# Gate's sizes taken in place while up runs, signed values by way of DRAM, first loads of u issued by ScalarE

## The reference, cut to what matters

```python
x = act_qdq(x)
up = act_qdq(x @ lpbq_dequant(w_up).T)
gate = act_qdq(x @ lpbq_dequant(w_gate).T)
sig = fixed_qdq_u16(sigmoid(gate))
gate = act_qdq(gate * sig)
o = act_qdq(gate * up)
return o @ lpbq_dequant(w_down).T
```

## Time and profile before

| | us |
|---|---|
| median of 3 runs | 1608.95 (1607.89 to 1610.02) |
| profiled execution | 1608.93 |
| its span | 1607.1 |
| PE busy | 1395.7 (87%) |
| VectorE busy | 1231.8 (77%) |
| ScalarE busy | 911.3 (57%) |
| moved by DMA | 200.56 MB, mean 125 GB/s |

### The profile page before, as it was taken

How to read it: one execution, slowest core, us unless ns; L and a number is a source line. 1 busy time by engine, 2 the same in 40 slices (tenths; PEclk the granted TensorE clock), 3 DMA queues, 4 the chain that set the end, 5 groups by cost and what they waited for, 6 DMA issues and landing times.

```text
span 1607.1 us, 24370 instructions
## 1 busy us (share of the span) xinstructions
PE 1395.7 (87%) x9268; PEld 788.3 (49%) x9268; DVE 1231.8 (77%) x1934; ACT 911.3 (57%) x1956; POOL 320.9 (20%) x326
## 2 busy tenths in 40 slices
PE   4579999999999999976999999999999203999999
PEld 3356666666666666642444444444444101444444
DVE  7657788888898988746888777688899799745641
ACT  2657787777777778755222222799844696321210
POOL 1124444444444444530111111000000000000000
PEclk9879999999999999978999999999999656999999
DMA  5101111111122221101233332577754995544532
GB/s 203 66 20 63 49 63 63 59 61 62 65 78 80 66 80 54 41 34 53 98 123 116 116 119 98 186 248 248 247 178 170 360 339 185 203 136 160 193 132 79
DMA packets 81812, 200.56 MB, mean 125 GB/s; under 512 B 7712, under 2 KB 7712, under 8 KB 78752
## 3 DMA queue, kind: packets, MB, share of 16 engines
q1 hardware_dynamic: 81696, 199.00, 35.4%
HBM read 128.72 MB, written 70.25 MB: 124 GB/s over the span
## 4 chain that ended last, share of the span: by engine, by line
PE 47%; issue 5%; DVE 1%; DMA 1%; ACT 0%; SPq 0%; POOLq 0%; POOL 0%
PE ffn_banks L1117 30%; PE ffn_banks L1135 16%; DMA ffn_ring<-sigs_dram 1%; PE ffn_banks L1093 1%; DVE ffn_wide L1283 0%; DVE ffn_rises L1288 0%; DVE ffn_peaks L1290 0%; DVE ffn_wide L1282 0%; ACT ffn_rest L1175 0%; ACT ffn_ring L1166 0%; DVE ffn_wide L1421 0%; DVE qg L1383 0%; ACT qg L1175 0%; SPq L1002 0%; PE ffn_banks L1123 0%
## 5 line engine op out<-in xcount | busy, mean ns | idle before, releaser
L1117 PE MATMUL ffn_banks<-ffn_wide,ffn_rest 128*128 128x512 f16 x2304 | 506.2, 381 | 10.4 <-DVE ffn_wide L1283 6.1
L1117 PEld LDWEIGHTS ffn_banks<-ffn_wide,ffn_rest 128*128 128x128 f16 x2304 | 226.1, 98 | 281.1 <-issue 17.3
L1135 PE MATMUL ffn_banks<-ffn_rest,ffn_wide 128*128 128x512 f16 x1152 | 251.2, 382 | 97.0 <-DVE ffn_wide L1428 97.0
L609 ACT ACTIVATE qg<-score_banks,neg_max 128x128 f32<-128x128 f32 (+1 forms) x512 | 207.6, 445 | 53.1 <-DVE neg_max L516 53.1
L1135 PEld LDWEIGHTS ffn_banks<-ffn_rest,ffn_wide 128*128 128x128 f16 x1152 | 113.2, 98 | 235.0 <-issue 100.7
L1175 ACT ACTIVATE ffn_rest<-ffn_banks,ffn_row_back 128x1024 f32<-128x1024 f32 x72 | 79.7, 1107 | 157.1 <-PE ffn_banks L1117 147.4
L1254 ACT ACTIVATE ffn_u_steps<-ffn_ring,ffn_scales 128x1024 int16<-128x1024 f32 x48 | 55.0, 1148 | 158.5 <-DMA ffn_ring<-ups_dram 131.2
L413 POOL TENSOR_TENSOR qg<-qg,per_sum 128x512 f32<-128x512 f32 x64 | 70.1, 1095 | 308.5 <-DVE per_sum L520 308.5
L415 POOL TENSOR_TENSOR qg<-qg,per_sum 128x1024 f32<-128x1024 f32 x64 | 121.1, 1892 | 0.0
L609 ACT ACTIVATION_READ_ACCUMULATOR qg<-score_banks,neg_max 128x1 f32 x512 | 118.9, 232 | 0.0
L657 PE MATMUL ring_banks<-xt,attn_hi 128*128 128x256 f16 x512 | 89.6, 277 | 10.3 <-DVE ct L501 6.3
(11 more groups left out here) (184 smaller groups left out, 2701.6 us busy)
## 6 DMA issues: line engine op xcount, KB each, us to landing
ups_dram<-ffn_rest SPq DMA_DIRECT2D x48, 512.0 KB, 3.1
ffn_ring<-ups_dram SPq DMA_DIRECT2D x48, 512.0 KB, 4.1
ffn_wide<-ups_dram SPq DMA_DIRECT2D x17, 1024.0 KB, 8.0
gates_dram<-ffn_rest SPq DMA_DIRECT2D x24, 512.0 KB, 2.7
ffn_ring<-gates_dram SPq DMA_DIRECT2D x24, 512.0 KB, 4.5
ffn_rest<-w_parts_dram SPq DMA_DIRECT2D x36, 256.0 KB, 4.0
x_in<-in_x SPq DMA_DIRECT2D x16, 512.0 KB, 3.7
qg<-in_ctxt SPq DMA_DIRECT2D x16, 512.0 KB, 4.2
```

What stands on the lines that cost most here:

```text
L609: last = act.activation(prob[:, s % 2, h, lo:hi], score_banks[:, h, lo:hi], ACT.Exp, bias=neg_max[:, s % 2, part, h:h + 1], accum_out=row_ ...
L1117: last = pe.matmul(banks[:, pair_of(s), half, :], w[:, m % 2, wp, c, :], xq[:, xp, n, c, :], start=(k == 0), stop=(k == 3 * DC - 1))
L1135: last = pe.matmul(down_banks[:, g % 2, t, :], oq[:, g % 2, op, m, t * P:(t + 1) * P], w_down[:, wp, wk, c], start=(start and k == 0), sto ...
```

## The change

`sizes` moves into the second pass and works in place on `qg`. A double's signed values are first stored to a new DRAM tensor, `signs` (`store_signed`, in SP's slot after the one in which the double's odd piece is made, ahead of that slot's fetches and of the store of up), and ScalarE takes the sizes one slot after that (`size_slots`). Double 23 keeps its signs and is the only one with two products. The signed values come back pair by pair and piece by piece (`load_signed`): those of the first two groups of down before it starts, the rest during groups 0, 2 and 4; VectorE's `multiply` waits for them (`a_back`). The ring of u has 9 places, since the size buffers' memory is free. Seven loads of u (`load_early`) are issued by ScalarE, in its slots 44 to 47, each once the piece of up that last reads the memory is filled; the other loads are SP's, and the down weights' loads stand between them. The doubles are taken even ones first.

```diff
...
 
 
 ND = NP // 2
-U_RING = 8
-FAR_PLACES = {0: 0, 1: 4, 2: 1, 3: 5, 6: 2, 7: 3}
-NEAR_PLACES = {4: 0, 5: 1}
+U_RING = 9
+FAR_PLACES = {0: 0, 1: 4, 2: 1, 3: 5, 4: 2, 5: 6, 8: 3}
+NEAR_PLACES = {6: 0, 7: 1}
 
 
 def unit_slot(u):
...
         w_raw = ring(8, 4, F32, "p (b t) -> p b t", b=2)
         w_deq = ring(12, 4, F32, "p (b t) -> p b t", b=2)
         parts = rest(16, 4, F16, "p (b s c o) -> p b s c o", b=2, s=2, c=DC)
-        far = wide(0, 48, F32, "p (b t) -> p b t", b=6)
+        far = wide(0, 56, F32, "p (b t) -> p b t", b=7)
         near = ring(0, 16, F32, "p (b t) -> p b t", b=2)
-        a_size = wide(48, 8, I16, "p (b t) -> p b t", b=2)
         u_more = wide(56, 8, I16, "p (b t) -> p b t", b=2)
         oq = wide(0, 48, F16, "p (g s m t) -> p g s m t", g=2, s=2, m=IC)
         y = wide(48, 8, F32, "p (t d) -> p t d", t=TG)
...
         sig2_ready, sig2_used, a_steps = sem("sig2_ready"), sem("sig2_used"), sem("a_steps")
         u_in = [sem(f"u_in{b}") for b in range(U_RING)]
         u_rounded, u_peaked, a_sized = sem("u_rounded"), sem("u_peaked"), sem("a_sized")
+        a_out = [sem(f"a_out{b}") for b in range(4)]
+        a_back = [[sem(f"a_back{q}_{j}") for j in range(2)] for q in range(PAIRS)]
         w_down_in = [sem(f"w_down_in{k}") for k in range(IC // DC)]
         du_in = [sem(f"du_in{b}") for b in range(4)]
         du_rounded, o_rounded, split = sem("du_rounded"), sem("o_rounded"), sem("split")
...
             k = stage_turn[s]
             eng.wait_ge(stored[k % 3], 16 * (k // 3 + 1))
 
-        double_order = [ND - 1] + list(range(ND - 1))
+        double_order = [ND - 1] + list(range(0, ND - 1, 2)) + list(range(1, ND - 1, 2))
+        signs_doubles = io["signs"].rearrange("m p (j c) -> m j p c", c=2 * W2)
+        signs_pairs = io["signs"].rearrange("(q a) p (j c) -> q j p a c", a=2, c=W2)
+        a_pairs = qg[:, :].rearrange("p (q a j c) -> p q j a c", a=2, j=PIECES, c=W2)
         doubles = qg[:, :].rearrange("p (d t) -> p d t", t=2 * W2)
 
-        def both_signs(k):
-            return k % 12 in (1, 3, 6, 8, 11)
-
-        sized = [k for k in range(ND) if not both_signs(k)]
-        signed = [k for k in range(ND) if both_signs(k)]
+        size_slots = [[] for _ in range(NP + 3)]
+        for c, t in [(c, t) for t in range(NP) for c in second[t]]:
+            if c % 2:
+                size_slots[t + 2].append(c // 2)
 
         def u_place(r):
             return near[:, NEAR_PLACES[r], :] if r in NEAR_PLACES else far[:, FAR_PLACES[r], :]
...
                     was_stored(sp, NP + c)
                 if k > U_RING:
                     sp.wait_ge(u_rounded, k - U_RING + 1)
-                elif r in NEAR_PLACES:
+                else:
                     sp.wait_ge(a_steps, NP)
-                else:
-                    sp.wait_ge(filled, 2 * NP - PIECES + 1 + FAR_PLACES[r] % 4)
                 sp.dma_start(u_place(r), up_doubles[d // 2, d % 2]).then_inc(u_in[r], 16)
+
+            def store_signed(d):
+                sp.wait_ge(a_steps, 2 * d + 2)
+                sp.dma_start(signs_doubles[d // 2, d % 2], doubles[:, d, :]).then_inc(a_out[d % 4], 16)
+
+            def load_signed(q, j):
+                last = max(double_order.index(2 * m + j // 2) for m in (2 * q, 2 * q + 1))
+                sp.wait_ge(u_peaked, last + 1)
+                for d in (4 * q + j // 2, 4 * q + 2 + j // 2):
+                    sp.wait_ge(a_out[d % 4], 16 * (d // 4 + 1))
+                sp.dma_start(a_pairs[:, q, j], signs_pairs[q, j]).then_inc(a_back[q][j % 2], 16)
 
             for b in range(2):
                 load_w(b)
...
                         load_gate(c)
                     if c % 2 and c >= 3:
                         spill(c - 2)
-                if t >= NP - 2:
-                    for k in range(2):
-                        load_again(1 + 2 * (t - NP + 2) + k)
+                for d in size_slots[t + 1]:
+                    store_signed(d)
                 for c in second[t]:
                     if c == 0:
                         spill(NP - 1)
...
                     if c % 2 and c >= 5:
                         fetch(c)
                 store_piece(s)
-            for k in range(5, ND):
+            for slot in size_slots[NP + 1:]:
+                for d in slot:
+                    store_signed(d)
+            for k in [7, 8] + list(range(10, 13)):
                 load_again(k)
+            for b in range(2):
+                sp.wait_ge(parts_stored[b], 16 * IC)
+            for b in range(3):
+                last = [k for k in range(len(stage_uses)) if k % 3 == b][-1]
+                sp.wait_ge(stored[b], 16 * (last // 3 + 1))
+            sp.wait_ge(u_rounded, 1)
             for m in range(IC):
-                if m == 0:
-                    sp.wait_ge(a_steps, NP)
-                    for b in range(2):
-                        sp.wait_ge(parts_stored[b], 16 * IC)
-                    for b in range(3):
-                        last = [k for k in range(len(stage_uses)) if k % 3 == b][-1]
-                        sp.wait_ge(stored[b], 16 * (last // 3 + 1))
                 k, r = divmod(m, DC)
                 unit = r * (IC // DC) + k
                 sp.dma_start(w_down_units[:, unit], io["w_parts"][2 * IC + unit]).then_inc(w_down_in[k], 16)
+            for k in range(13, ND):
+                load_again(k)
+            for q in range(PAIRS):
+                load_signed(q, 0)
 
             def load_u(g, q):
                 r = g * PAIRS + q
                 if r < 4:
-                    sp.wait_ge(u_rounded, ND - 2 + r // 2)
+                    sp.wait_ge(u_rounded, 17 + r // 2)
                 else:
                     sp.wait_ge(du_rounded, r - 3)
                 sp.dma_start(du[:, r % 4], up_pairs[g, q]).then_inc(du_in[r % 4], 16)
...
                 for q in range(PAIRS):
                     if g < NG:
                         load_u(g, q)
+                    if g < 2 * (PIECES - 1) and g % 2 == 0:
+                        load_signed(q, g // 2 + 1)
                     if g >= 2 and q == 0:
                         for t in range(TG):
                             load_x2(g - 2, t)
...
                         act.activation(parts[:, u % 2, 0].rearrange("p c o -> p (c o)"), banks[:, 3, u % 2, :],
                                        ACT.Copy).then_inc(w_hi, 1)
 
+            def sizes(d):
+                act.wait_ge(a_out[d % 4], 16 * (d // 4 + 1))
+                act.activation(doubles[:, d, :], doubles[:, d, :], ACT.Abs).then_inc(a_sized, 1)
+
+            def load_early(k):
+                r, d = (k - 1) % U_RING, double_order[k]
+                for c in (2 * d, 2 * d + 1):
+                    was_stored(act, NP + c)
+                act.dma_start(u_place(r), up_doubles[d // 2, d % 2]).then_inc(u_in[r], 16)
+
             act.wait_ge(u_backed, 1)
             for t in range(NP):
                 evacuate(NP + t)
+                for k in range(1, U_RING + 1):
+                    if k - 1 in FAR_PLACES and t == NP - PIECES + FAR_PLACES[k - 1] % 4:
+                        load_early(k)
                 for c in first[t]:
                     if c == 0:
                         act.wait_ge(g_scaled, 1)
...
                         act.wait_ge(sig2_used, c // 2 - 1)
                     act.activation(chain[:, c % 4, :], steps_of_piece[:, c, :], ACT.Sigmoid,
                                    scale=sc["g_step"]).then_inc(sig2_ready, 1)
-
-            def sizes(n):
-                if n >= 2:
-                    act.wait_ge(u_peaked, sized[n - 2] + 1)
-                act.activation(a_size[:, n % 2, :], doubles[:, double_order[sized[n]], :], ACT.Abs).then_inc(a_sized, 1)
-
-            act.wait_ge(a_steps, NP)
-            act.wait_ge(filled, 2 * NP)
-            sizes(0)
-            sizes(1)
+                for d in size_slots[t]:
+                    sizes(d)
+
+            late = [d for slot in size_slots[NP:] for d in slot if d != ND - 1]
             act.wait_ge(u_scaled, 1)
             for k in range(ND):
                 if k == 0:
...
                     src = u_place(r)
                 if k >= 3:
                     act.wait_ge(u_peaked, k - 2)
-                if k in sized[2:]:
-                    sizes(sized.index(k))
                 act.activation(u_of(k), src, ACT.Abs, scale=sc["u_per"]).then_inc(u_rounded, 1)
+                if 0 <= k - 4 < len(late):
+                    sizes(late[k - 4])
 
             for r in range(NG * PAIRS):
                 act.wait_ge(du_in[r % 4], 16 * (r // 4 + 1))
...
             dve.tensor_tensor(sc["o_unit"], sc["a_step"], sc["u_step"], ALU.mult).then_inc(u_scaled, 1)
             dve.wait_ge(a_steps, NP)
             for k in range(ND):
+                d = double_order[k]
                 dve.wait_ge(u_rounded, k + 1)
-                if both_signs(k):
-                    n = signed.index(k)
-                    a = doubles[:, double_order[k], :]
-                    if n > 0:
```

(18 more changed lines are left out.)

## The result

Five runs of the changed kernel gave a median of 1617.27 us (1612.9 to 1619.52) against 1607.89 of before, also the median of five; the ratio is 1.0061, 95% interval 1.0038 to 1.0084: slower by some 10 us (0.6%), where 1611 was forecast (range 1596 to 1626, chance of slower 0.43). The profiled execution took 1617.1 us, its span 1615.3.

The account below looks back on a forecast made before the run. The time was taken as up matmuls, hole and down matmuls, only the hole able to shrink. Loop -23.9, second pass +24.9 and loads +1.5 gave +2.5 us on 1608.9, so 1611 us, range 1596 to 1626.

Parts of the forecast that it names:

- The loop in the hole: Between up and down matmuls: 25 products instead of 34, first down matmul at X + 63.5 instead of 87.4, -23.9 us.
- X: The moment the last signed piece a ends, 1265.3 us before the change; forecast to move by +24.9 us.
- Sizes while up runs: ScalarE in up: moved size operations add 2.2 us a slot, 4.6 of 5.2 us in all, hidden.
- The store ahead of the fetch: SP's slots in up's second pass: fetches 0.85 us late at 18 gaps, 15.3 us, plus 3.6 for slow landings.
- slow landings: Fetches behind a store in up's second pass: the slow kind, +1.8 us, counted twice, 3.6 us.
- The early loads: ScalarE's seven loads late in up's second pass: beside four gaps, 3 us each, 12 us.
- the even share: Two queues beside the early loads share 400 GB/s evenly: store and fetch take 2 us more; 3 a gap taken.
- Together: Up's second pass: fetch and other waits of 30.9 us after against 6.0 before, so X moves by +24.9 us.
- Loads at the start of down: Loads in the loop and the first u pair before down: +1.5 us, bounds 0 to 3.
- The balance: Whole kernel, likeliest case, chance 0.40: -23.9, +24.9 and +1.5 sum to +2.5 us; 1604 to 1618 us.
- The rival in which the early loads starve SP's queue: Four gaps, slots 43 to 47: row-by-row sharing makes landings 6.2 us later, 25 us for 12; 1624 us, chance 0.24.

Follow-up runs that it names:

- e3: The changed kernel without stores and loads of the signed values; sizes wait for the piece itself and down multiplies by sizes: 1585.62 us, a single execution.
- e1: The changed kernel with SP issuing each slot's fetches first and the store of the signed double behind them: 1593.42 us, 0.9920 of before.
- e2: The kernel before, with only the stores of signed doubles added ahead of the fetches, read by nobody: 1628.76 us, 1.0140 of before.
- e8: The changed kernel with fetches ahead of the signed store, and signed and u pairs loaded in turn before down: 1590.99 us, 0.9901 of before.
- e5: The changed kernel with each of ScalarE's seven early loads issued as four DMAs of 512 columns (2 KB rows): 1613.13 us, a single execution.
- e6: The changed kernel with fetches ahead of the signed store, early loads in 2 KB rows, signed and u pairs in turn: 1591.53 us, 0.9895 of before.

## Why the prediction was right or wrong

- *The loop in the hole: right.* VectorE starts at X + 3.5 and the last product ends at 1353.2, X + 59.1, forecast 59.0. 25 products, without a gap between them. e3 gives the 63.5 us from X to down by themselves.
- *Sizes while up runs: right as to the time, with one thing unseen.* PE has no gap in up, VectorE lost nothing to it (e3). But ScalarE waits 30.8 us for signed stores to land; VectorE never waited for it in the second pass, but it set the moments of the early loads.
- *The store ahead of the fetch: right in kind, a little low in size.* The forecast had 0.85 us at each gap and 3.6 for slow landings, for the 14 gaps away from the early loads 15.5 in all; 15 such gaps took 18.1, each 0.84 to 1.59, mostly 1.0, and one slow one 2.83. This term was mis-sized by 2.6 us. The sum had a landing in 3.3 us, and the chain shows most between 3.4 and 3.9 and one of 5.41, where two slow ones were counted. e1 and e2 show the mechanism from both sides.
- *The early loads: the sum nearly right, its parts not.* It had four gaps of 0.85 + 3 us, 15.4. There were three, of 5.56, 5.46 and 5.30, 16.3; over a quiet gap's 1.0 each costs 4.4 us where the forecast took 3. What failed is the even share from which the 3 came: SP's queue moved nothing until about 4 us after the issue of the store, then about a third, and the fetch landed behind both loads, 7.9 to 8.1 us after its issue. The rule of turns a packet at a time, from which the prediction reasoned that a fetch does not stand behind all the loads, fits only the stretch after that. The fourth gap that the sum had was free of this (1.59 us). That the whole came near is in part luck: too many gaps at too low a price.
- *Together:* waits 34.4 for 30.9, X moved by 28.8 for 24.9. This is 3.9 of the 5.7 us that the profiled difference (8.2) lies above the forecast's 2.5.
- *Loads at the start of down: too low.* +1.5 within bounds of 0 to 3; 66.1 - 63.5 = 2.6 us came. e8 wins 3.2 by taking the pairs in turn. Down itself took 0.6 more, which the forecast had at 0.
- *The balance:* the forecast laid the two halves, +24.9 and -23.9, against each other and gave slower 0.43. The likeliest value was 6 us low, inside the range. The rival in which the early loads starve SP's queue has the right sign, and the queue did starve at the start of each burst, but at 4.4 us over three gaps, 13 us, and not at 6.2 over four, 25; and its reason, row sizes, isn't what makes the waits (e5). The Trainium skill says that issuing from several engines saves issue time only (DMA: Bandwidth & Descriptors, Issuing engines are not separate DMA queues). The runs agree in so far as the second queue gained nothing: with SP issuing the same loads the hole is 100.4 us for 106.2, and 81.9 for 82.1 with the fetches first, neither clear of the scatter.

## What to carry to other kernels

In a queue written out by hand, a wait counts for everything behind it: a store that needs the newest result, put ahead of a prefetch that needs an older one, takes a step of the prefetch's depth away. Here two blocks exchanged turned 10 us of loss into 13 of gain. Count for each prefetch what must be done before it is issued, and compare issue and landing with the work that its consumer has left; a load begun early delays the small, urgent transfers behind it, on whichever queue, so set that cost (14 us ahead of X here) against what it saves later (17 us).

## What the runs showed that I had not expected

A load queue of its own, fed by a compute engine that waits for landings, was no better than the one shared queue (hole 106.2 against 100.4, not clear of the scatter). Two loads begun 2 us ahead on ScalarE's queue kept SP's queue from moving anything for 3.7 to 4.0 us after the issue of its store (2.5 to 3.7 us with quarter rows); only after that did the two queues exchange packet for packet. And issuing the loads in four parts cost ScalarE up to 5.7 us at a time in front of its next sigmoid (e6).
